# One pass of 2048 columns for each head product, where two passes of 1024 stood, on the vector engine

## What is computed

```python
h = _rmsnorm(x, gamma1)
q = (h @ Wq + bq).reshape(b, t, H, HD)                       # H = 16, HD = 8
kv = ((h @ Wdown + bdown) @ Wup + bup).reshape(b, t, H, 2 * HD)
k, v = jnp.split(kv, 2, axis=-1)
att = jnp.einsum('bthd,btgd->bthg', q, k) / np.sqrt(HD)       # 16 x 16 for each token
att = jax.nn.softmax(att, axis=-1)
out = jnp.einsum('bthg,btgd->bthd', att, v).reshape(b, t, D)
```

## Time and profile before

| | |
|---|---|
| time before, median of 3 runs | 6333.34 us (6317.61 to 6354.56) |
| the profiled execution | 6351.87 us, of it 6350.3 us span |
| PE busy | 4773.4 us, 75% |
| DVE busy | 3599.9 us, 57% |
| POOL busy | 2177.1 us, 34% |
| ACT busy | 1800.9 us, 28% |
| half sums (L1281 and L1284) | 288 of 1.21 us |

### The profile page before, as it was taken

How to read it: one execution, slowest core, us unless ns; L and a number is a source line. 1 busy time by engine, 2 the same in 40 slices (tenths; PEclk the granted TensorE clock), 3 DMA queues, 4 the chain that set the end, 5 groups by cost and what they waited for, 6 DMA issues and landing times. The chain is left out here.

```text
span 6350.3 us, 94963 instructions
## 1 busy us (share of the span) xinstructions
PE 4773.4 (75%) x36264; PEld 2844.7 (45%) x36264; DVE 3599.9 (57%) x10874; ACT 1800.9 (28%) x2589; POOL 2177.1 (34%) x2704
## 2 busy tenths in 40 slices
PE   5879797979787887858767767677677776876773
PEld 3444545444545353533544535435344354353452
DVE  3545555555555555547466575474665754746654
ACT  2424242424232333323113132231231322312310
POOL 1323131313131313546135252261342522614425
PEclk9989898989898888877768877787788777887886
DMA  4000000000000001640000000000000000000000
GB/s 145 7 16 7 15 8 15 11 12 11 12 11 12 15 8 49 197 150 7 9 19 3 13 13 6 16 7 10 18 5 12 12 6 17 7 11 17 5 13 4
DMA packets 142049, 147.57 MB, mean 23 GB/s; under 512 B 31150, under 2 KB 126064, under 8 KB 141064
## 3 DMA queue, kind: packets, MB, share of 16 engines
q1 hardware_dynamic: 114424, 94.58, 5.0%
q0 software_dynamic: 18432, 37.79, 2.0%
q10 hardware_dynamic: 8736, 8.91, 0.4%
HBM read 70.75 MB, written 62.59 MB: 21 GB/s over the span
## 5 line engine op out<-in xcount | busy, mean ns | idle before, releaser
L787 DVE CUSTOM_DVE_ANT_0 twin<-twin,w_mask_row 128x512 f32<-128x512 f32 (+3 forms) x2048 | 953.3, 520 | 384.9 <-PE twin L1711 381.9
L1711 PE MATMUL twin<-arena 32*128 32x128 f32 (+3 forms) x4096 | 835.9, 537 | 54.3 <-DVE arena L787 25.1
L1729 PE MATMUL twin<-arena 32*128 32x128 f32 (+3 forms) x4096 | 788.5, 506 | 46.1 <-DVE arena L787 44.1
L1408 ACT ACTIVATE arena<-twin 128x768 f32<-128x768 f32 (+1 forms) x544 | 477.8, 882 | 718.7 <-PE twin L1740 387.5
L1729 PEld LDWEIGHTS twin<-arena 32*128 32x128 f32 x4096 | 361.6, 205 | 487.7 <-issue 290.9
L690 POOL TENSOR_SCALAR ve<-mv 128x4 f32<-128x4 f32 x128 | 27.7, 216 | 1549.1 <-DVE mv L747 1548.6
L1711 PEld LDWEIGHTS twin<-arena 32*128 32x128 f32 x4096 | 370.6, 213 | 235.5 <-issue 127.6
L316 POOL DMA_INDIRECT got<-sorted_y,back x288 | 285.4, 991 | 551.3 <-ACT arena L1589 278.1
L308 POOL DMA_INDIRECT sorted_x<-got,w_mo_first_slots x288 | 282.4, 980 | 486.1 <-DVE ring L861 320.6
L1664 PE MATMUL twin<-w_ident,b 128*128 128x128 f32 x328 | 91.1, 433 | 388.1 <-DVE b L768 337.2
L1752 PE MATMUL twin<-arena 128*32 128x128 f32 (+3 forms) x2944 | 305.4, 460 | 2.9 <-POOL arena L592 2.9
(11 more groups left out here) (440 smaller groups left out, 10435.1 us busy)
## 6 DMA issues: line engine op xcount, KB each, us to landing
sorted_y<-arena SPq DMA_DIRECT2D x96, 256.0 KB, 2.7
sorted_x<-zeros ACTq DMA_DIRECT2D x2, 4096.0 KB, 20.0
a<-sorted_x SPq DMA_DIRECT2D x64, 128.0 KB
b<-sorted_x SPq DMA_DIRECT2D x64, 128.0 KB, 2.4
hres<-sorted_x SPq DMA_DIRECT2D x64, 128.0 KB
sorted_x<-got,w_mo_first_slots POOLq DMA_INDIRECT x288
got<-sorted_y,back POOLq DMA_INDIRECT x288
x_out<-w_l_w SPq DMA_DIRECT2D x18, 256.0 KB, 2.3
```

Of the source, the lines that this page charges most:

```text
L787: last = dve.tensor_tensor_reduce(s[:, e, at:at + w], s[:, e, at:at + w], W["mask_row"][:, T - w:T], -1.0, 3e38, ALU.add, ALU.min, into)
L1408: act.activation(at_pt[tag][n % len(at_pt[tag])][:, :, 0:w], twin[SLOT["scores_t", c, u] % 3][:, :, 0:w], ACT.Exp, scale=1.0 if tag == "l1 ...
L1711: last = pe.matmul(s[:, e, at:at + w], queries[r, P * i:P * (i + 1)], keys[r, 0:w], start=(at == 0), stop=True, skip_group_check=True)
L1729: last = pe.matmul(s[:, e, at:at + w], keys[r, P * m:P * (m + 1)], queries[r, P * m:T], start=(at == 0), stop=(tag == "l2"), skip_group_ch ...
```

## The change

`take(m)` sums a whole product in one instruction of 2048 columns and raises `f_read` behind it. Its steps are those at which the second half stood, so what was done at steps 0 and 2, or 4 and 5, of a quartet is done at 2, or 5.

```diff
-                        def take(m, half):
+                        def take(m):
                             phase, q, t = m // (2 * NT), m // NT % 2, m % NT
                             dve.wait_ge(sg["f_pool"], m + 1)
-                            heads = slice(H // 2 * half, H // 2 * (half + 1))
                             if phase == 0:
-                                i = dve.tensor_reduce(ht_sc[q][:, t, heads], ht_pr[m % 2].rearrange(
-                                    "p (h g d) -> p h g d", h=H, g=H)[:, heads], AX, ALU.add)
+                                i = dve.tensor_reduce(ht_sc[q][:, t], ht_pr[m % 2].rearrange(
+                                    "p (h g d) -> p h g d", h=H, g=H), AX, ALU.add)
...
-                            if half == 1:
-                                i.then_inc(sg["f_read"], 1)
+                            i.then_inc(sg["f_read"], 1)
...
-TAKE_STEP = {(-2, 3): (0, 0), (-2, 4): (0, 1), (-1, 0): (1, 0), (-1, 1): (1, 1), (-1, 2): (2, 0), (-1, 3): (2, 1),
-             (-1, 5): (3, 0), (0, 0): (3, 1)}
+TAKE_STEP = {(-2, 4): 0, (-1, 1): 1, (-1, 3): 2, (0, 0): 3}
 for c_ in range(HEAD_QUARTETS):
-    TAKE_STEP[c_ + 1, 0], TAKE_STEP[c_ + 1, 2] = (4 + 2 * c_, 0), (4 + 2 * c_, 1)
-    TAKE_STEP[c_ + 1, 4], TAKE_STEP[c_ + 1, 5] = (5 + 2 * c_, 0), (5 + 2 * c_, 1)
+    TAKE_STEP[c_ + 1, 2], TAKE_STEP[c_ + 1, 5] = 4 + 2 * c_, 5 + 2 * c_
```

More of the change, by code:

```diff
@@ L1082, in beside @@
                                 if (c, u) in TAKE_STEP:
-                                    take(*TAKE_STEP[c, u])
+                                    take(TAKE_STEP[c, u])
                                 if (c, u) == (0, 1):
@@ L1273, in l3_front @@
                                                   ALU.add).then_inc(sg["f_q"], 1)
-                        def take(m, half):
+                        def take(m):
                             phase, q, t = m // (2 * NT), m // NT % 2, m % NT
                             dve.wait_ge(sg["f_pool"], m + 1)
-                            heads = slice(H // 2 * half, H // 2 * (half + 1))
                             if phase == 0:
-                                i = dve.tensor_reduce(ht_sc[q][:, t, heads], ht_pr[m % 2].rearrange(
-                                    "p (h g d) -> p h g d", h=H, g=H)[:, heads], AX, ALU.add)
-                            else:
-                                i = dve.tensor_reduce(ht_o[q][:, t].rearrange("p (h d) -> p h d", h=H)[:, heads],
-                                                      ht_pr[m % 2].rearrange("p (h d g) -> p h d g", h=H, d=DH)[:, heads],
+                                i = dve.tensor_reduce(ht_sc[q][:, t], ht_pr[m % 2].rearrange(
+                                    "p (h g d) -> p h g d", h=H, g=H), AX, ALU.add)
+                            else:
+                                i = dve.tensor_reduce(ht_o[q][:, t].rearrange("p (h d) -> p h d", h=H),
+                                                      ht_pr[m % 2].rearrange("p (h d g) -> p h d g", h=H, d=DH),
                                                       AX, ALU.add)
-                            if half == 1:
-                                i.then_inc(sg["f_read"], 1)
+                            i.then_inc(sg["f_read"], 1)
                         def head_maxima(q):
@@ L1367, in finish_alone @@
                             for m in range(2 * NT):
-                                take(m, 0)
-                                take(m, 1)
+                                take(m)
                             for q in PAIR:
```

## The result

The changed kernel takes 6393.93 us (median; 6380.17 to 6408.57), the one before in the same series 6353.84 us (6317.61 to 6378.81). The ratio is **1.0073, with a 95% interval of 1.0048 to 1.0098**: slower by 0.7%, some 46 us. The forecast was 6342 us with a range of 6308 to 6372; the result lies above it. The forecast had counted from 6333.34 us, the median of three runs; the six runs have 6353.84, so some 20 us of the distance to 6342 are that base. The rest, some 31 us, is the change: by the medians it cost 40 us (46 by the ratio) and not 9. The profiled execution took 6397.26 us, 45.4 more than that of before.

A forecast was written before the change was run, and what follows sets the result against it. DVE and POOL were taken as both close to full, PE third. Terms made six rounds 1.1 us longer, rounds 1 and 5 1.3 each, the last part 0.1 shorter: 9 us more, 6342 us, range 6308 to 6372.

The forecast's parts named there:

- Rival D: Merged pass no cheaper than two halves: 5 us more from the sums, 6347 us; chance 0.05.
- rival A: DVE is the bound and POOL doesn't bite: eight rounds gain 22 us, 6311 us; chance 0.22.
- Term 1: Steps (-2, 3) to (0, 1): four merged sums, 0.2 us gained.
- Term 2: Shifts (0, 1) to (1, 1) and (1, 1) to (2, 1): 0.5 us gained in each.
- Term 4: Shifts (3, 1) to (4, 1): DVE's idle 1.59 us filled by 1.07 us of sum, 0.5 us gained.
- Term 3: Shifts (2, 1) to (3, 1): product 9 ends later, the head maxima's subtraction waits for it, 1.05 us lost.
- Term 5: Shifts (4, 1) to (5, 1): products 12 and 13 come later, head outputs end behind 13, 0.7 us lost.
- Term 6: Shifts (5, 1) to (6, 1): one pass of 2.2 us replaces two halves, 0 to 0.1 us gained.
- rule of the place: A whole sum at the second half's step ends 1.07 us later counted from the shift, delaying the product waiting for it.
- Term 7: Round's end: product 15 waits for the whole sum, masks of quartet 6 queue behind it, 1.05 us lost.
- rival B: PE stays longer at clock 0.50 after its wait at (3, 2) in six short rounds: 35 us more, 6377 us; chance 0.13.

The follow-up runs named there:

- f2: Changed kernel plus one to three matmuls that nobody reads in PE's stalls; ratio 1.0032 to the kernel before, 6371.32 us.
- f0: The changed kernel run once more, unedited, beside the runs with unread matmuls; ratio 1.0064 to the kernel before, 6386.69 us.
- e1: Changed kernel with two halves of 1024 columns back to back where its one pass stands; ratio 1.0057 to the kernel before, 6389.98 us.
- e4: Changed kernel's one pass per product, but at the steps of the first halves, 0 and 4; ratio 1.0082 to the kernel before, 6398.33 us.
- g2: Kernel before with products 4 + 2c behind POOL's masks of step 3, not of step 1; ratio 0.9992, 6342.87 us.
- m2: Changed kernel with head work behind the shift, a third product buffer, and POOL's product held until the subtraction is done; ratio 0.9814 to the kernel before.
- k2: Kernel before with a third product buffer, so POOL waits only for the sum of product m - 3; ratio 1.0006, 6352.34 us.
- m1: k2 with POOL holding its product back until the subtraction of the head maxima is done; ratio 0.991 to the kernel before, 6314.48 us.

## Why the prediction was wrong, point by point

- *The merged pass* costs 2.278 us, the forecast's 2.27. Rival D fell, and rival A too.
- *Terms 1, 2 and 4.* Term 1, 0.2 us gained, didn't come (17.1 stays). By the prediction's own words the maxima at (0, 1) wait for product 4 in any case: the subtraction got shorter, 2.78 us for 3.84, and ends 1.08 us behind that product in both kernels. Term 2: to (1, 1) 0.6 to 1.4 us were gained in seven rounds, not 0.5, and 2.0 lost in round 5; to (2, 1) 12.8 against the forecast 12.7, in rounds 5 and 6, where the clock held, and 15.1 to 15.3 in the six others. Term 4 came in rounds 6 and 7 only, and there as 15.3 to 15.6 (15.8); the others took 16.9 to 19.0. Timeline of DVE, after, round 3, maxima of (3, 3) and (3, 5):

```profile
3790.84 0.56 DVE L787 CUSTOM_DVE_ANT_0 twin<-twin,w_mask_row 128x384 f32<-128x384 f32 x1 [0.64 <-PE twin L1707]
...
3796.47 0.43 DVE L787 CUSTOM_DVE_ANT_0 twin<-twin,w_mask_row 128x256 f32<-128x256 f32 x1 [1.77 <-PE twin L1707]
```

  The idle time ahead of step 3 went from 1.59 us to 0.64, as forecast (under 0.7), and came back as 1.77 ahead of step 5, which a half at step 4 had covered. I had asked what the longer sum fills and not what the removed half had filled.
- *Term 3*, the subtraction behind the later product 9, held in both mechanism and size in three rounds: 17.7 to 17.8 us (17.7 forecast); it was 18.5 or so in five. The instruction itself takes 1.93 to 3.11 us, and 2.85 in the round shown (3.2 forecast; 2.32 before). Timelines of DVE and POOL, after, round 3:

```profile
3783.55 2.85 DVE L1293 TENSOR_TENSOR w_mo_wgu<-w_mo_wgu 128x1024 f32<-128x1024 f32 x1
3786.33 0.67 DVE L811 TENSOR_TENSOR arena<-arena,twin 128x512 f32<-128x512 f32 x1
...
3771.78 5.48 POOL L646 TENSOR_TENSOR w_mo_wgu<-w_mo_wgu,w_l_cs_feat 128x2048 f32<-128x2048 f32 x1 [1.11 <-DVE w_mo_wgu L1280]
...
3779.11 5.49 POOL L646 TENSOR_TENSOR w_mo_wgu<-w_mo_wgu,w_l_cs_feat 128x2048 f32<-128x2048 f32 x1
3784.51 0.82 POOL L592 TENSOR_SCALAR_AFFINE_SELECT ring<-ring 128x256 f32<-128x256 f32 x2
```

  As in the earlier trace rows POOL has no gap from product 8 to product 9. Here the two masks behind product 9 took 0.82 us where they took 1.78, and the subtraction ended 1.80 us behind the product, not 1.08 (the prediction read 1.15): this time the masks came first, a piece the prediction left out. It separates all eight rounds: 1.08 us behind the product in the three of 17.7 to 17.8, 1.80 in the five of 18.5.
- *Term 5*: 17.2 to 17.6 in rounds 5 to 8 (17.3 forecast), 18.0 to 18.8 in rounds 1 to 4.
- *Term 6* is the term that was **mis-sized by mechanism**: "0 to 0.1 us gained" to (6, 1), measured 14.0 to 14.8 for 12.8 in six rounds, a loss of 1.2 to 2.0 us (12.7 and 16.7 in the other two), with the filler too (13.8 to 14.8 in f2). I had followed DVE's row there and not product 14, which by my own rule of the place starts a microsecond later, with the masks of (6, 0) and PE's values behind it.
- *Term 7*: the waits of PE for masks, after, round 3, which answer (0.35 us) and the earlier trace rows (2.08 us):

```profile
3778.03 0.52 PE L1748 MATMUL twin<-arena 128*32 128x384 f32 x2 [1.43 <-POOL arena L592]
...
3843.40 0.94 PE L1748 MATMUL twin<-ring,arena 128*32 128x512 f32 x2 [3.09 <-POOL ring L592]
```

  That is 1.43 us at (3, 0), 1.08 later as the rule of the place says, and 3.09 us at (6, 4), the forecast's 3.1, with a tail of 29.3 for 29.2. Over the rounds the tail is 24.1 to 30.2. But the matmul behind it takes 0.94 us where it took 0.62: PE comes back at the low clock.
- *The step that failed* is the choice of the likeliest case: that the six short rounds keep their pattern of clocks while their stalls move, with 0.50 for it and 0.13 for rival B. It put the clock's cost at nothing. In its place the runs showed rounds at 0.77 to 0.84 and 38.1 us more in the stretches, of which the filler alone gives back 28 (f2 against f0). The prediction also put the pieces between the rounds at nothing and the last part at 0.1 us gained; they took 15.4 and 6.9 us more, with a clock of 0.64 for 0.86 in `l3_front`. The number that came is B's, 1.0073 x 6333 = 6380 us against its 6377, but that agreement is partly luck: B had its loss from (3, 2) on, and the clock falls at (1, 2) too, behind a *shorter* stall, and outside the stretches, which B didn't count. The prediction itself counted 5.9 us for each round that loses its pattern, against 1.1 for the sum of all seven terms. With such a ratio the chance of B decides the forecast, and I put it at 0.13 with "two of eight rounds do it already" as the evidence. Six rounds alike to 0.1 us are no sign that the pattern holds under a change: each of e1 to e4 breaks it, and so does g2, where the 21 us gained at (0, 1) make up for it.
- *Not settled*: why the clock falls in one round and holds in another behind the same stall (2.27 us in rounds 1 and 2 of the kernel before, 1.79 us in rounds 3 and 6 of the changed one). The filler shows that PE's idle time has a part in it; which idle time at which moment, no run here isolates. Nor does any run show how the moved sums lower the clock in `l3_front`, over 220 us behind them.

The rule of the Trainium skill that the prediction weighed (SBUF — State Buffer, "Who interferes with whom") is borne out further than it was used there. The rows show that whichever starts first keeps going: 6.36 us for the subtraction behind a product that started 0.05 us earlier, 6.02 behind one that started 0.40 earlier (e4), 6.43 us for the product behind a subtraction that started 0.39 us earlier. The page says the same, that the order of issue decides who blocks; by that rule, the traces agree.

## What to carry to other kernels

When instructions move between steps of a schedule with three tight engines, follow each of them through the *other* engine's queue to the last thing queued there (here: sum, product, masks, values, shift), for every place it moves in, and give the case "the clock pattern breaks" the weight of its price. If a buffer's release is what ties two engines, a third buffer makes the place of the release nearly free (0.993 with the late sums here, 0.991 with the early halves once the race is gone). And where two engines exclude each other, let the long instruction wait for the short one by a semaphore: in m2 1.5 us of POOL bought 5 us of DVE.

## What the runs showed of the hardware

- A subtraction of two SBUF inputs (1.23 us alone) takes 6.36 us when a product of POOL starts 0.05 us before it, and 1.48 when it starts 0.39 us ahead of the product. Which of the two happens can turn on a change elsewhere in the round: it hid the gain of the third buffer in k2 altogether (sum 1109.3, and 1024.0 in m1), and lengthened e4's subtractions by 28 us in all.
- PE's granted clock was 0.60 and 0.54 over 8 us in which PE was busy all the time, behind a stall of 1.79 us, and 1.00 behind one of 2.27 us; in other rounds it was the other way round with the same two stalls. One to three matmuls that nobody reads in each stall brought the changed kernel's rounds to 0.85 to 0.90, where they had 0.77 to 0.84, and the kernel before no time at all (0.9992 [0.9969, 1.0015]).
- PE's clock can be lost far from the change: the same matmuls without a gap took 9.38 us at 0.86 and 12.34 us at 0.64, over 220 us behind the last moved sum.
- A sum of 2048 columns in one pass is 2.278 us, two of 1024 back to back 2.34: 0.06 us for one instruction less. Merging 144 such passes took 4.7 us off DVE's work; their place cost some 46 us.
